# Retention in chunks of 64 tokens on 64x64 tiles of the array, with the inner and the state products issued apart

## Chip, cores and metric

One core of a Trainium2 chip runs the program. The metric is the device time in microseconds of one execution. TensorE (PE, its weight loads PEld), VectorE (DVE), ScalarE (ACT), GpSimd (POOL) and SyncE (SP) each run a queue of their own; the queues meet at semaphores only.

## The reference

Four sequences of 1024 tokens with 1024 features. Of the normalized rows `xn` it computes a retention layer with 16 heads of 64, and a linear layer whose input and weights are rounded to 4 bits in blocks of 16, and adds both to `x`:

```python
q = heads((x @ Wq + bq) * scaling); k = heads(x @ Wk + bk); v = heads(x @ Wv + bv)
D = jnp.where(causal[None], jnp.exp(decay[:, None, None] * diff_c[None]), 0.0)
ret = jnp.einsum('bhid,bhjd->bhij', q, k) * D[None]
scale = jnp.clip(jnp.abs(jax.lax.stop_gradient(ret).sum(-1, keepdims=True)), 1.0, None)
attn = jnp.einsum('bhij,bhjd->bhid', ret / scale, v)
...
g = (g - mu) / jnp.sqrt(var + EPS)      # per head, over its 64 features
g = g.reshape(b, s, e) * gn_w + gn_b
gate = jax.nn.silu(x @ Wg + bg)
return gate * g @ Wo + bo
...
x = x + attention(xn) + ffn(xn)
```

Since the weight of a pair of tokens decays by a constant factor per token, the sum over earlier tokens can be split: tokens of the same chunk are multiplied out (scores, then inner products with v), and all tokens of earlier chunks enter through a 64x64 state per head that is decayed and increased by each chunk (state products).

## The kernel before

The 4096 tokens are cut into 8 groups of 512, a group into 4 chunks of 128 (CH). The weights are in pairs of heads: 8 pairs, 128 features each. A **body** computes two pairs (u = 0, 1) of one group, and the output rows and the next group's input of one chunk. There are 2 + 2 bodies of the phases FIRST_A and FIRST_B (together group 0), 4 of SECOND (group 1), 24 of MIDDLE (groups 2 to 7) and 4 of TAIL. Every group has 4 bodies. `parity` is the group's number modulo 2; groups with parity 0 begin a sequence, and their first chunk has no state before it.

In a body PE runs, for each pair, four projections (`project`, L1145: k, v, q and g, n = 0 to 3, each 24 matmuls of 512 columns in f16 parts, into the PSUM banks mm0 and mm1 in turn), transposes of k and v (`transpose_kv`, L1159), the scores (L1167, 24 f16 matmuls of 128x128 blocks with 64 rows of contraction, one head in each half of the rows), the state increments (L1178, f32, k decayed times v with a column of ones), and `attend` (L1190): the state products (L1203, q times the state before the chunk) and the inner products (L1207, masked scores times v) into the same banks `ao`. P(u,n) below is the projection n of pair u. `transpose_g` (L1122, Tg below) transposes the group-normalized output. From group 1 on there are also `finish_half` (L1093, the output projection of the group before, 24 matmuls) and in MIDDLE `finish_linear` (L1114, 8 matmuls).

The other engines, in the order of their queues in a body:

- ACT (L651 to L679): copies of k(0) and v(0) out of mm (`evacuate`, L593, lines L604 and L606), `decay_k(0)`, `x_hi`, copy of q(0), `copy_v(0)`, g(0), k(1), v(1), `decay_k(1)`, `normalize(0)` (L632, line L637), q(1), `copy_v(1)`, g(1), `affine(0)` (L642, line L647), `normalize(1)`, `affine(1)`. `affine(1)` waits for Tg of pair 1, which PE issues in the next body, `transpose_g(1, 1)` at L1215.
- DVE (L991 to L1037): layer norm and quantizing of one input chunk, `mask_scores(0)` (L929), `states(0)` (L938), `group_norm(0)` (L954), `mask_scores(1)`, `states(1)`, the output additions, `group_norm(1)`, output additions.
- POOL: `split` (L450) makes the second f16 part of k and q, `decay_q`, `gate_y`.
- SP issues all DMAs: one slice of weights ahead of each projection, inputs, outputs and transposing DMAs.

The order is written out by hand, and all waits are counts in the table PER. `group_norm(u)` waits for `attn_full`, which the last matmul of `attend` raises; `normalize(u)` waits for `gstats`; scores(1) waits for `kq_split`, which POOL raises after q(1) has been copied by ACT; `transpose_kv(0, "k")` waits for `mm0_free`, raised by ACT's second copy of k.

Of the kernel before, what the change touches and what calls it, by code (L numbers as in the profile page):

```python
# [52 lines left out]
VW = HD + 1  # L53
BLK = 16
# [24 lines left out]
    "attn_full": (1, 2, 2, 2, 2, 0), "gstats": (0, 2, 2, 2, 2, 0), "normed": (1, 2, 2, 2, 2, 0),  # L79
# [13 lines left out]
    "step": (85, 74, 74, 120, 76, 0),  # L93
# [53 lines left out]
def build(nc, a):  # L147
    with ExitStack() as ctx:
# [15 lines left out]
        dmask = sb("dmask", [P, HEADS, P])  # L164
# [22 lines left out]
        state = sb("state", [P, CH, VW])  # L187
# [47 lines left out]
        bias_sum = ctx.enter_context(nc.semaphore("bias_sum"))  # L235
        v_ones = ctx.enter_context(nc.semaphore("v_ones"))
# [16 lines left out]
        late_res = probs[:].rearrange("p a b c -> p (a b c)")  # L253
        block = ctx.enter_context(nc.Block())
# [6 lines left out]
        def _(sp):  # L261
# [19 lines left out]
            for dst, name in ((ident[:], "ident"), (dec_h[:], "dec_h"),  # L281
                              (dec_c[:], "dec_c"), (work[:, 0:P], "ages"), (xa[:, 0:P], "causal"),
# [235 lines left out]
        def _(act):  # L518
# [4 lines left out]
            for h in range(HEADS):  # L523
                nc.scalar.activation(dmask[:, h, :], work[:, 0:P], ACT.Exp, scale=dec_h[:, h:h + 1])
# [3 lines left out]
            nc.scalar.activation(lam[:], dec_c[:], ACT.Exp, scale=float(P)).then_inc(tables, 1)  # L528
# [157 lines left out]
        def _(dve):  # L686
# [196 lines left out]
            then(V.tensor_scalar(xa[:, 0:P], xa[:, 0:P], kq_down["k"], kq_down["q"], ALU.mult, ALU.mult))  # L883
            V.tensor_scalar(kfac[:], kfac[:], kq_down["k"], None, ALU.mult)
            V.tensor_scalar(qfac[:], qfac[:], kq_down["q"], None, ALU.mult)
            then(V.tensor_tensor(dmask[:], dmask[:], xa[:, 0:P].unsqueeze(1).broadcast_to([P, HEADS, P]), ALU.mult))
# [22 lines left out]
            def body(phase, i, parity, q, group):  # L909
# [19 lines left out]
                def mask_scores(u):  # L929
                    w("scores_full", u + 1)  # L930
                    w("attn_full", u)
                    for h in range(2):
                        factor = dmask[:, ds(q * 4 + 2 * u + h, 1), :].broadcast_to([P, CH, P])
                        last = V.tensor_tensor(probs[:, h], sc[h].rearrange("p (c t) -> p c t", c=CH), factor,  # L934
                                               ALU.mult)
                    last.then_inc(s["probs_ready"], 1)

                def states(u):  # L938
# [5 lines left out]
                    if parity == 0:  # L944
                        then(V.tensor_copy(state[:, 1], tp[bk][:, 0:VW]))
# [5 lines left out]
                    V.scalar_tensor_tensor(pair, state[:, CH - 1], decay, tp[bk][:, (CH - 1) * VW:CH * VW],  # L951
# [46 lines left out]
                if phase == SECOND:  # L998
                    f_scales(0)
                    f_half(0)  # L1000
# [309 lines left out]
```

## Time and profile before

| | us |
|---|---|
| median of 3 runs | 2363.78 (2360.42 to 2365.61) |
| the profiled execution's own time | 2367.02 |
| its span, first to last instruction | 2365.2 |
| PE busy | 2186.9 (92%) |
| DVE busy | 1451.8 (61%) |
| ACT busy | 672.8 (28%) |
| POOL busy | 635.1 (27%) |

The profile's page has busy times by engine, a row of 40 slices, the chain that ended last and the costliest groups of instructions. Two more views are used: windows, which give the same numbers for chosen stretches with the granted clock of TensorE (PEclk, 1.00 is 2.4 GHz, 0.50 is 1.2 GHz), and the timeline, which lists the instructions of an engine with their start, their duration, and in brackets how long the engine had been idle before and what released it. An f32 matmul leaves two records. Durations of matmuls overlap, so a rate is read from one start to a later start.

### The profile page before, as it was taken

Reading aid. Unit: us, or ns where it says so; the run is one execution under the profiler, and the core shown is the slowest. Engines: PE = TensorE matmul, PEld = TensorE weight load, DVE = VectorE, ACT = ScalarE, POOL = GpSimd, SP = SyncE. Lnnn points to the kernel's source line nnn. Section 1 sums busy time; section 2 is a strip of 40 time slices with the busy share of each in tenths; the row PEclk is TensorE's granted clock in tenths of the full one; section 3 lists DMA queues with packets and bytes.
Section 4 is the critical chain, followed back from the end, with each engine's and each line's share of the span. In section 5 each row is a group of like instructions: output and inputs, shape, how many; then the busy total and the mean of one; then the engine's idle time right before and its main releaser. Section 6 shows DMA issues by size and latency. Waiting matters only on the chain.

```text
span 2365.2 us, 42202 instructions
## 1 busy us (share of the span) xinstructions
PE 2186.9 (92%) x13472; PEld 1158.0 (49%) x13472; DVE 1451.8 (61%) x4086; ACT 672.8 (28%) x1259; POOL 635.1 (27%) x460
## 2 busy tenths in 40 slices
PE   1289797988889999999999999999999999999999
PEld 1044453544445555555555555555555555555554
DVE  7766576887974555666655555666655556666532
ACT  4534332222222223222222223222222223222220
POOL 1022232222222233223222233232222233232321
PEclk9689899898989999999999999999999999999999
DMA  7964333234323233333233233333233233333233
GB/s 284 368 202 148 94 114 104 85 98 126 104 76 103 86 105 111 103 103 102 82 96 103 83 108 111 103 103 102 77 101 102 81 111 111 103 102 99 78 102 116
DMA packets 189396, 271.20 MB, mean 115 GB/s; under 512 B 118288, under 2 KB 139280, under 8 KB 188304
## 3 DMA queue, kind: packets, MB, share of 16 engines
q1 hardware_dynamic: 189328, 270.35, 36.6%
q8 instruction: 36, 0.59, 0.1%
q14 instruction: 32, 0.26, 0.0%
HBM read 203.20 MB, written 37.75 MB: 102 GB/s over the span
## 4 chain that ended last, share of the span: by engine, by line
PE 79%; DVE 13%; issue 2%; SPq 2%; ACT 2%; DMA 1%; POOL 0%; DVEq 0%; ACTq 0%; POOLq 0%
PE mm L1154 48%; PE mm L1101 6%; PE tp L1101 6%; PE four L1207 5%; PE mm L1110 4%; PE four L1203 3%; PE tp L1164 2%; PE four L1174 2%; PE tp L1186 1%; SPq L277 1%; PE tp L1128 1%; DVE xm L753 1%; DVE xa L750 1%; DVE xa L755 1%; DVE xa L751 1%
## 5 line engine op out<-in xcount | busy, mean ns | idle before, releaser
L1154 PE MATMUL mm<-xnT,wring 128*128 128x512 f16 x6144 | 1391.4, 384 | 47.8 <-ACT qT L606 15.5
L1154 PEld LDWEIGHTS mm<-xnT,wring 128*128 128x128 f16 x6144 | 604.7, 99 | 753.9 <-issue 54.3
L637 ACT ACTIVATE work<-four,gs 128x64 f32<-128x64 f32 x512 | 158.0, 414 | 545.5 <-DVE gs L976 545.5
L934 DVE TENSOR_TENSOR probs<-four,dmask 128x512 f32<-128x512 f32 x128 | 82.5, 686 | 325.5 <-PE four L1174 324.2
L470 POOL TENSOR_TENSOR yT<-gn,gate 128x512 f32 x64 | 81.2, 1269 | 659.3 <-ACT gn L647 659.3
L453 POOL TENSOR_TENSOR qparts<-qT,qparts 128x512 f16<-128x512 f32 x64 | 79.8, 1247 | 657.0 <-ACT qT L606 657.0
L963 DVE BATCH_NORM_STATS2 gst<-four 128x6 f32<-128x64 f32 x512 | 73.6, 217 | 230.3 <-PE four L1207 229.5
L1101 PE MATMUL mm<-wo,yT 128*128 128x512 f16 x864 | 192.6, 379 | 0.0
L1101 PE MATMUL tp<-wo,yT 128*128 128x512 f16 x672 | 149.6, 379 | 0.0
L453 POOL TENSOR_TENSOR kparts<-kT,kparts 128x512 f16<-128x512 f32 x64 | 76.8, 1199 | 224.6 <-ACT kT L606 209.5
L1207 PE MATMUL four<-v,probs 128*128 128x65 f32 x1024 | 136.7, 290 | 0.0
L1207 PEld LDWEIGHTS four<-v,probs 128*128 128x128 f32 x1024 | 127.6, 203 | 4.6
L1101 PEld LDWEIGHTS mm<-wo,yT 128*128 (+1 forms) x864 | 82.2, 98 | 96.5 <-POOL yT L473 0.4
L606 ACT ACTIVATE vT<-mm,bias,cols 128x512 f32<-128x512 f32 x64 | 49.7, 777 | 238.1 <-PE mm L1154 238.1
L606 ACT ACTIVATE gate<-mm,bias,cols 128x512 f32<-128x512 f32 x64 | 49.7, 777 | 193.9 <-PE mm L1154 193.9
L1101 PEld LDWEIGHTS tp<-wo,yT 128*128 (+1 forms) x672 | 66.1, 100 | 73.6
L755 DVE TENSOR_TENSOR xa<-xa,xm 128x512 f32<-128x512 f32 x80 | 100.4, 1255 | 2.8
L1203 PE MATMUL four<-state,qT 64*128 64x65 f32 x896 | 68.0, 291 | 35.4 <-DVE carry L951 35.4
L1110 PE MATMUL mm<-wf,xqT 128*128 128x512 bf16 x416 | 98.3, 379 | 0.0
L604 ACT ACTIVATE kparts<-mm,bias,cols 128x512 f16<-128x512 f32 x64 | 49.5, 773 | 168.7 <-PE four L1174 168.6
L647 ACT ACTIVATE gn<-tp,gnp 128x512 f32<-128x512 f32 x64 | 49.5, 773 | 161.1 <-PE tp L1128 161.1
L621 ACT ACTIVATE kn<-tp,kfac 128x256 f32<-128x256 f32 x128 | 53.4, 470 | 132.8 <-PE tp L1164 132.8
(174 smaller groups left out, 2483.5 us busy)
## 6 DMA issues: line engine op xcount, KB each, us to landing
wring<-parts SPq DMA_DIRECT2D x256, 512.0 KB, 3.4
xt<-in_x SPq DMA_DIRECT2D x34, 512.0 KB, 4.3
out<-res SPq DMA_DIRECT2D x32, 512.0 KB, 2.9
res<-in_x SPq DMA_DIRECT2D x28, 512.0 KB, 3.5
parts<-xqT SPq DMA_DIRECT2D x36, 256.0 KB, 4.4
parts<-xnT SPq DMA_DIRECT2D x36, 256.0 KB, 3.5
ftile<-in_w_f SPq DMA_DIRECT2D x16, 512.0 KB, 4.3
yT<-in_w_k SPq DMA_DIRECT2D x1, 4096.0 KB, 14.8
```

The lines of the kernel that those rows point to most:

```text
L453: nc.gpsimd.tensor_tensor(parts[:, 1], full[:], parts[:, 0], ALU.subtract)\
L470: nc.gpsimd.tensor_tensor(hi, gn[:], gate[:, u], ALU.mult)
L606: nc.scalar.activation(dst, mm[n % 2][:], ACT.Silu if n == 3 else ACT.Identity, bias=bias[:, n, pair(u)], scale=down[MATS[n]])\
L637: last = nc.scalar.activation(work[:, c * P + h * HD:c * P + (h + 1) * HD], ao[h][:, c * VW:c * VW + HD], ACT.Identity, bias=gs[:, 1, g:g ...
L755: then(V.tensor_tensor(xa[:], xa[:], xm[:], ALU.add))
L934: last = V.tensor_tensor(probs[:, h], sc[h].rearrange("p (c t) -> p c t", c=CH), factor, ALU.mult)
L963: last = V.bn_stats(gst[:, g, :], ao[h][:, c * VW:c * VW + HD])
L1101: last = MM(out[:], y[:, yj, k, ds(q * P, P)], wo[:, wj, k, h * GROUP:(h + 1) * GROUP], start=(n == 0), stop=(n == 3 * KT - 1))
L1110: last = MM(out, xs[:, k, :], wf[:, k, h * GROUP:(h + 1) * GROUP], start=(k == 0), stop=(k == KT - 1))
L1154: last = MM(mm[n % 2][:], wring[:, slot, wj, k, :], xnT[:, parity, xj, k, :], start=(j == 0), stop=(j == 3 * KT - 1))
L1203: MM(ao[h][:, columns(c)], qT[r, c * P:(c + 1) * P], state[r, c], start=(c == earlier[0]), stop=False, skip_group_check=True)
L1207: last = MM(ao[h][:, columns(c)], probs[:, h, c, :], v1[:, c, h, :], start=False, stop=True, skip_group_check=True)
```

## The change

The chunk of the attention shrinks from 128 to 64 tokens (SUB, 8 per group), while all copies keep their layout of 128. Scores, masks, increments, state products and inner products all use 64x64 tiles: two token halves times two heads. The inner products and the state products become two functions, `attend_within` and `attend_earlier`, which raise `within` and `attn_full`. Half of the increments are written to the free half of the banks of the scores, so they wait for the mask (`probs_ready`). PE's order changes: P(0,1) precedes the transposes of g of the body before, the increments and inner products of pair 0 follow P(1,1), its state products follow P(1,2); in pair 1 the scores precede the output half, and the state products follow the second output half. On DVE the recurrence has 8 steps, and in SECOND and FIRST the mask and the states change places with parts of the weight quantizing. ACT's and POOL's queues keep their order.

```diff
-        dmask = sb("dmask", [P, HEADS, P])
+        dmask = sb("dmask", [P, HEADS, SUB])
...
+        def increment(bk, k):
+
+            c = k // 2
+            if k % 2 == 0:
+                return tp[bk][:, c * VW:(c + 1) * VW]
+            first = CH * SUB + c % 2 * VW
+            return sc[c // 2][:, first:first + VW]
...
-                    for c in range(1 if parity == 0 else 0, CH - 1):
-                        then(V.scalar_tensor_tensor(state[:, c + 1], state[:, c], decay, tp[bk][:, c * VW:(c + 1) * VW],
+                    for k in range(1 if parity == 0 else 0, SUBS - 1):
+                        then(V.scalar_tensor_tensor(state[:, k + 1], state[:, k], decay, increment(bk, k),
                                                     ALU.mult, ALU.add))
...
+                mask_scores(0)
+                if phase == SECOND:
                     f_half(0)
-                mask_scores(0)
-                states(0)
                 if phase in FIRST:
                     find_f_max(0)
+                states(0)
...
                 def scores(u):
                     w("kq_split", 2 * u + 2)
                     w("probs_ready", u)
+                    pe.sem_inc(pe_turn, 1)
                     for c in range(CH):
-                        for h in range(2):
-                            r, t = slice(h * HD, (h + 1) * HD), slice(c * P, (c + 1) * P)
-                            for kj, qj in ((0, 0), (0, 1), (1, 0)):
-                                last = MM(sc[h][:, t], kparts[r, kj, t], qparts[r, qj, t],
-                                          start=(kj + qj == 0), stop=(kj == 1))
+                        for kj, qj in ((0, 0), (0, 1), (1, 0)):
+                            for par in range(2):
+                                for h in range(2):
+                                    r, out = slice(h * HD, (h + 1) * HD), slice(par * SUB, (par + 1) * SUB)
+                                    at_t = slice(c * P + par * SUB, c * P + (par + 1) * SUB)
+                                    last = MM(sc[h][out, c * SUB:(c + 1) * SUB], kparts[r, kj, at_t],
+                                              qparts[r, qj, at_t], start=(kj + qj == 0), stop=(kj == 1))
...
+                    w("probs_ready", u + 1)
+                    pe.sem_inc(pe_turn, 1)
+                    for k in range(SUBS):
+                        rows, c = slice(k % 2 * SUB, (k % 2 + 1) * SUB), k // 2
                         for h in range(2):
-                            last = MM(tp[bk][h * HD:(h + 1) * HD, c * VW:(c + 1) * VW], kn[:, c, h, :], v1[:, c, h, :],
+                            last = MM(increment(bk, k)[h * HD:(h + 1) * HD], kn[rows, c, h, :], v1[rows, c, h, :],
                                       start=True, stop=True)
...
+                def attend_within(u):
+                    w("normed", u)
+                    pe.sem_inc(pe_turn, 1)
+                    for k in range(SUBS):
+                        for h in range(2):
+                            last = MM(ao[h][tokens(k), columns(k)], probs[tokens(k), h, k // 2, 0:SUB],
+                                      v1[tokens(k), k // 2, h, :], start=(k < 2), stop=False, skip_group_check=True)
+                    last.then_inc(s["within"], 1)
+
+                def attend_earlier(u):
                     w("qdec_ready", u + 1)
...
+                    for k in range(1 if parity == 0 else 0, SUBS):
                         for h in range(2):
                             r = slice(h * HD, (h + 1) * HD)
+                            last = MM(ao[h][tokens(k), columns(k)], qT[r, k * SUB:(k + 1) * SUB], state[r, k],
                                       start=False, stop=True, skip_group_check=True)
                     last.then_inc(s["attn_full"], 1)
...
                 project(0, 0)
+                project(0, 1)
                 if last_g:
                     transpose_g(1, 1)
-                project(0, 1)
                 transpose_kv(0, "k", kT, 0)
...
                 scores(0)
+                project(1, 1)
                 state_increments(0)
-                project(1, 1)
-                attend(0)
+                attend_within(0)
                 transpose_kv(1, "k", kT, 0)
                 project(1, 2)
+                attend_earlier(0)
                 transpose_kv(1, "v", vT, 1)
-                project(0 if phase in FIRST else 1, 3)
-                transpose_g(0)
+                if phase in FIRST:
+                    scores(1)
+                    project(0, 3)
+                    state_increments(1)
+                    attend_within(1)
+                    project(1, 3)
+                    transpose_g(0)
+                    attend_earlier(1)
+                    return
+                project(1, 3)
                 scores(1)
-                state_increments(1)
-                if phase in FIRST:
-                    project(1, 3)
-                    attend(1)
-                    return
                 pe.wait_ge(s["y_ready"], group * (2 * CH) + 1)
                 finish_half(w, parity, q, 0, "mm0", 5)
+                transpose_g(0)
+                state_increments(1)
+                attend_within(1)
                 if phase == MIDDLE:
                     finish_linear(w, parity, q, 0, "mm1", 5)
-                attend(1)
-                if phase == MIDDLE:
                     finish_half(w, parity, q, 1, "t1", 4)
-                    finish_linear(w, parity, q, 1, "mm1", 6)
                 else:
                     finish_half(w, parity, q, 1, "mm1", 5)
+                attend_earlier(1)
+                if phase == MIDDLE:
+                    finish_linear(w, parity, q, 1, "mm1", 6)
```

How the rows of PE move. The start of a MIDDLE body before (`work` is the normalized output that Tg transposes, `xnT,wring` a projection; ISA and REGISTER_ALU rows compute the counts waited for):

```order
L1154 MATMUL mm<-xnT,wring 128x512 x24
L257 ISA
L257 REGISTER_ALU
L1128 MATMUL tp<-ident,work 128x128 x4
L257 REGISTER_ALU
L257 ISA
L1154 MATMUL mm<-xnT,wring 128x512 x24
L257 REGISTER_ALU x2
L1164 MATMUL tp<-ident,kT 128x128 x4
```

and of the change:

```order
L1169 MATMUL mm<-xnT,wring 128x512 x24
L269 REGISTER_ALU
L269 ISA
L1169 MATMUL mm<-xnT,wring 128x512 x24
L269 ISA
L269 REGISTER_ALU
L1143 MATMUL tp<-ident,work 128x128 x4
L269 REGISTER_ALU x2
L1179 MATMUL tp<-ident,kT 128x128 x4
L1169 MATMUL mm<-xnT,wring 128x512 x24
```

The transposes of g (L1128, now L1143) stood between the two projections and now stand directly ahead of those of kT.

Pair 0 of a MIDDLE body from its state products on, before (scores(1), L1174, come next):

```order
L1203 MATMUL four<-state,qT 128x65 x8
L1207 MATMUL four<-v,probs 128x65 x8
L257 REGISTER_ALU
L1164 MATMUL tp<-ident,kT 128x128 x4
L1154 MATMUL mm<-xnT,wring 128x512 x24
L257 REGISTER_ALU
L1164 MATMUL tp<-ident,vT 128x128 x4
L257 REGISTER_ALU
L1154 MATMUL mm<-xnT,wring 128x512 x24
L257 REGISTER_ALU
L1128 MATMUL tp<-ident,work 128x128 x4
L257 REGISTER_ALU
```

and the same place of the change, from the inner products on:

```order
L1219 MATMUL four<-v,probs 64x65 x16
L269 REGISTER_ALU
L1179 MATMUL tp<-ident,kT 128x128 x4
L1169 MATMUL mm<-xnT,wring 128x512 x24
L269 REGISTER_ALU
L1232 MATMUL four<-state,qT 64x65 x16
L269 REGISTER_ALU
L1179 MATMUL tp<-ident,vT 128x128 x4
L269 REGISTER_ALU
L1169 MATMUL mm<-xnT,wring 128x512 x24
L269 REGISTER_ALU
L1192 MATMUL four<-qparts,kparts 64x64 x48
```

The state products (L1203, now L1232) stood ahead of the inner products and of the projection of q(1); now they follow that projection, and between them and scores(1) only vT and one projection are left.

## Rows read from the trace of the kernel before

**Rows 1.** The page, section 1, busy time by engine, share of span, instructions.
```profile
PE 2186.9 (92%) x13472; PEld 1158.0 (49%) x13472; DVE 1451.8 (61%) x4086; ACT 672.8 (28%) x1259; POOL 635.1 (27%) x460
```

**Rows 2.** Windows: stretch, length, busy time by engine (x instructions), PEclk, DMA share, GB/s.
```profile
365.00:689.40 324.40, 274.72 (x1623) 148.43 (x1621) 259.46 (x680) 76.98 (x156) 80.87 (x57) 0.89 0.33 99
689.40:2290.00 1600.60, 1600.60 (x10078) 848.66 (x10079) 930.61 (x2791) 444.00 (x885) 462.22 (x336) 1.00 0.33 98
...
1041.41:1108.24 66.83, 66.83 (x426) 35.54 (x424) 39.66 (x118) 18.55 (x38) 19.29 (x14) 1.00 0.33 98
...
1308.27:1374.65 66.38, 66.38 (x418) 35.12 (x416) 38.51 (x118) 18.55 (x38) 19.28 (x14) 1.00 0.33 99
```

**Rows 3.** Timeline of PE, a FIRST body: start, us, engine, line, count, [idle before].
```profile
311.99 0.66 PE L1128 MATMUL tp<-ident,work 128*128 128x128 f32 x4 [2.52 <-ACT work L637]
```

**Rows 4.** Timeline of PE, pair 0 of one MIDDLE body.
```profile
1051.71 0.85 PE L1174 MATMUL four<-qparts,kparts 64*128 64x128 f16 x24
1052.49 0.69 PE L1186 MATMUL tp<-v,kn 128*64 128x65 f32 x16
1053.11 5.35 PE L1154 MATMUL mm<-xnT,wring 128*128 128x512 f16 x24
1058.39 1.11 PE L1203 MATMUL four<-state,qT 64*128 64x65 f32 x16
1059.43 2.00 PE L1207 MATMUL four<-v,probs 128*128 128x65 f32 x16
1061.27 0.61 PE L1164 MATMUL tp<-ident,kT 128*128 128x128 f32 x4
1061.71 5.34 PE L1154 MATMUL mm<-xnT,wring 128*128 128x512 f16 x24
1066.89 0.60 PE L1164 MATMUL tp<-ident,vT 128*128 128x128 f32 x4
...
1073.04 0.85 PE L1174 MATMUL four<-qparts,kparts 64*128 64x128 f16 x24
```

**Rows 5.** Timelines of PE and ACT, start of the next body.
```profile
1096.41 0.60 PE L1128 MATMUL tp<-ident,work 128*128 128x128 f32 x4
...
1097.16 0.78 ACT L647 ACTIVATE gn<-tp,gnp 128x512 f32<-128x512 f32 x1 [5.36 <-PE tp L1128]
1097.84 0.77 ACT L604 ACTIVATE kparts<-mm,bias,cols 128x512 f16<-128x512 f32 x1
1098.50 0.77 ACT L606 ACTIVATE kT<-mm,bias,cols 128x512 f32<-128x512 f32 x1
```

**Rows 6.** Timelines of DVE, ACT and POOL, between the pairs.
```profile
1061.46 1.15 DVE L963 BATCH_NORM_STATS2 gst<-four 128x6 f32<-128x64 f32 x8 [5.82 <-PE four L1207]
...
1066.27 2.47 ACT L637 ACTIVATE work<-four,gs 128x64 f32<-128x64 f32 x8 [3.42 <-DVE gs L976]
1068.59 0.82 ACT L604 ACTIVATE qparts<-mm,bias,cols 128x512 f16<-128x512 f32 x1
...
1070.15 1.16 POOL L453 TENSOR_TENSOR qparts<-qT,qparts 128x512 f16<-128x512 f32 x1 [12.40 <-ACT qT L606]
```

**Rows 7.** Timeline of PE and windows, around three idles in SECOND.
```profile
644.90 1.97 PE L1203 MATMUL four<-state,qT 64*128 64x65 f32 x16 [4.25 <-DVE carry L951]
...
527.58 5.35 PE L1154 MATMUL mm<-xnT,wring 128*128 128x512 f16 x24 [2.03 <-DVE res L1045]
...
604.89 1.65 PE L1154 MATMUL mm<-xnT,wring 128*128 128x512 f16 x6 [2.03 <-DVE res L1045]
...
643.60:653.80 10.20, 8.90 (x43) 7.04 (x44) 8.06 (x33) 0.84 (x2) 0.00 (x0) 0.50 0.31 78
...
527.60:531.00 3.40, 3.40 (x16) 1.56 (x17) 3.23 (x7) 1.64 (x6) 0.00 (x0) 1.00 0.38 154
...
604.90:609.50 4.60, 4.60 (x14) 1.80 (x15) 4.36 (x9) 1.65 (x6) 0.00 (x0) 0.63 0.28 114
```

**Rows 8.** Groups of DVE by line: busy us, mean ns | idle before.
```profile
L949 DVE SCALAR_TENSOR_TENSOR state<-state,lam,tp 128x65 f32<-128x65 f32 x160 | 45.1, 282 | 14.3 <-DVE state L945 4.7 <-DVE state L947 3.1 <-DVE state L949 0.2
```

More of the change, by code:

```diff
@@ L53 @@
 VW = HD + 1
+SUB = 64
+SUBS = GROUP // SUB
 BLK = 16
@@ L91 @@
     "w_k": (2, 2, 2, 2, 2, 0), "w_v": (2, 3, 3, 2, 2, 0), "w_q": (2, 2, 2, 2, 2, 0), "w_g": (2, 1, 1, 2, 2, 0),
-    "step": (85, 74, 74, 120, 76, 0),
+    "step": (85, 82, 82, 128, 84, 0),
 }
@@ L186, in build @@
         probs = sb("probs", [P, 2, CH, P])
-        state = sb("state", [P, CH, VW])
+        state = sb("state", [P, SUBS, VW])
         gn = sb("gn", [P, GROUP])
@@ L523, in _ @@
             for h in range(HEADS):
-                nc.scalar.activation(dmask[:, h, :], work[:, 0:P], ACT.Exp, scale=dec_h[:, h:h + 1])
+                nc.scalar.activation(dmask[:, h, :], work[:, 0:SUB], ACT.Exp, scale=dec_h[:, h:h + 1])
             for r in range(PAIRS):
@@ L1012, in body @@
                 mask_scores(1)
-                states(1)
+                if phase == SECOND:
+                    f_half(0)
                 if phase == FIRST_B:
                     split_o_lo(i, 1, w)
-                if phase == SECOND:
-                    f_half(0)
+                states(1)
                 if phase == MIDDLE:
@@ L1116, in finish_linear @@
                 w(f"{bank}_free", use - 1)
+                pe.wait_ge(s["xqf_moved"], at("xqf_moved", MIDDLE, 0, 0))
                 linear(banks[bank][:], parity, q, h).then_inc(s[f"{bank}_full"], 1)
@@ L1191, in attend @@
+                def attend_earlier(u):
                     w("qdec_ready", u + 1)
-                    w("probs_ready", u + 1)
                     b, n = uses[f"u{u}"]
                     w(f"t{b}_free", n)
-                    w("normed", u)
-                    earlier = [c for c in range(CH) if not (parity == 0 and c == 0)]
-                    columns = lambda c: slice(c * VW, (c + 1) * VW)
-                    for c in earlier:
+                    w("within", u + 1)
+                    pe.sem_inc(pe_turn, 1)
+                    for k in range(1 if parity == 0 else 0, SUBS):
@@ L1201, in attend @@
                         for h in range(2):
                             r = slice(h * HD, (h + 1) * HD)
-                            MM(ao[h][:, columns(c)], qT[r, c * P:(c + 1) * P], state[r, c],
-                               start=(c == earlier[0]), stop=False, skip_group_check=True)
-                    for c in range(CH):
-                        for h in range(2):
-                            last = MM(ao[h][:, columns(c)], probs[:, h, c, :], v1[:, c, h, :],
+                            last = MM(ao[h][tokens(k), columns(k)], qT[r, k * SUB:(k + 1) * SUB], state[r, k],
@@ L1253, in _ @@
             run_phase(pe, SECOND, body)
-            pe.wait_ge(s["xqf_moved"], at("xqf_moved", MIDDLE, 0, 0))
             run_phase(pe, MIDDLE, body)
@@ L1277 @@
     idx = np.arange(P)
+    sub = idx % SUB
     decay = g[p + "decay"]
@@ L1293 @@
         "ident": np.eye(P, dtype=f32),
-        "ages": np.maximum(idx[None, :] - idx[:, None], 0).astype(f32),
-        "causal": (idx[None, :] >= idx[:, None]).astype(f32),
-        "pos": np.broadcast_to(idx.astype(f32), (P, P)).copy(),
-        "left": (P - idx).astype(f32).reshape(P, 1),
+        "ages": np.maximum(sub[None, :SUB] - sub[:, None], 0).astype(f32),
+        "causal": (sub[None, :SUB] >= sub[:, None]).astype(f32),
+        "pos": np.broadcast_to(sub.astype(f32), (P, P)).copy(),
+        "left": (SUB - sub).astype(f32).reshape(P, 1),
     }
```

24 lines of the change are left out of this document (13 added, 11 removed).

## The prediction

> **What bounds the kernel now.** I read the page first, then stretches, then one body instruction by instruction. TensorE is busy 92% of the span [rows 1]. By stage [rows 2]: from 689.4 us to 2290.0 us (the 24 MIDDLE bodies) PE is busy for all of its 1600.60 us at clock 1.00, and DVE for 58%. One body takes 66.83 us (odd groups) or 66.38 us (even), 66.6 in the mean. So in MIDDLE every microsecond of PE work counts fully, and so does every wait that PE is made to take. In the four SECOND bodies (most of 365.0 to 689.4) PE is busy 274.72 of 324.40 us and DVE 259.46: there DVE and PE wait for each other. In the FIRST bodies PE waits for ACT, as at 311.99 [rows 3].
>
> The sum is made against the profiled execution, 2367.0 us with a span of 2365.2; it stands 3.2 us above the median of 2363.8. A difference of 0.2% (some 5 us) is about what a measurement here can tell from none.
>
> **The attention products.** The timeline of PE in one body [rows 4] gives what a pair costs. A projection without a change of tile shape takes 5.18 us (1061.71 to 1066.89), so the one begun at 1053.11 is through at 1058.29, and the state products start at 1058.39: a change of tile shape costs 0.10. From start to next start: scores 0.78 for 24 records, increments 0.62 for 16, state products 1.04 for 16, inner products 1.84 for 16 (an f32 matmul leaves two records). The first three include one change of shape each, and there are two more, going into scores and into the state products: 4.28 + 0.20 = 4.48 us a pair, of which 0.5 are five changes and 3.98 is work.
>
> That work runs in steps. Scores use two 64-row tiles at once: 12 steps of 0.057. Increments use two 64-column tiles at once: 8 steps of 0.065. State products, two 64-row tiles with 128 columns of weights: 8 steps of 0.118. Inner products, the whole array with 128 columns of weights: 16 steps of 0.115. The step follows the weight columns, not the rows.
>
> The change makes 48, 32, 32 and 32 records, 144 for 72. All have 64 columns of weights. No row has four tiles at once, so it is bounded. Taken: four tiles work abreast where the code addresses four in turn, and a step costs what the nearest row with 64 weight columns shows. Scores 12 x 0.057 = 0.68; increments 8 x 0.065 = 0.52 (as many as before, with twice the records and twice the tiles); state products 8 x 0.065 = 0.52; the inner products only ever use the two tiles on the diagonal, 16 x 0.065 = 1.04. Together 2.76, and six changes of shape for five (there are three stretches of 64x64 tiles a pair, each entered from and left to the 128x128 shape): 0.60. 3.36 for 4.48 saves 1.12 us a pair, **2.2 us a body**. The lower end of the cost is every step halved once more, 1.4 + 0.6 = 2.0 (5 us saved a body). The upper end is that no record comes faster than the closest ones do now, scores with 0.68/24 = 0.028 us: 144 x 0.028 + 0.6 = 4.6, nothing saved.
>
> The Trainium skill, TensorEngine Tiling (Array Packing), section Instruction Overhead, speaks against such small pieces: about 60 cycles for each matmul whatever its width, and a tiling factor should not be taken from a side that is already small. Estimated from that page, 60 cycles at 2.4 GHz are 25 ns, so 144 records would take 3.6 us and the sum would save 0.3 us a pair in place of 1.1; no row here has narrow tiles four abreast to settle it.
>
> **The transposes of g, moved behind P(0,1).** Before, Tg (L1128) stands between the first two projections. ACT must then run affine and both copies of k before PE may transpose kT, because they stand in this order in its queue, and the queue is not changed. The rows [rows 5]: Tg from 1096.41, 0.44 long for PE; affine 1097.16, kparts 1097.84, kT from 1098.50 to 1099.27. That ran under the second projection. Now kT's transposes follow Tg at once: they could start at Tg's start + 0.44 and are allowed 1099.27 - 1096.41 = 2.86 later at the earliest. Idle **2.5 us** a body with the hand-over. Nothing else covers it: the ACT queue is strictly ordered, and affine cannot precede Tg.
>
> **The state products of pair 0, moved behind P(1,2).** They now carry attn_full, on which group norm waits. ACT holds normalize(0) ahead of the copies of q of pair 1, these release POOL's split, and scores(1) waits for the split. This chain [rows 6], from the end of the attention at 1061.27 (kT's start, [rows 4]): group norm 1061.46, normalize 1066.27, q copies from 1068.59, split 1070.15 to 1071.31, **10.04 us**. Before, PE had kT, P(1,2), vT, P(1,3) and Tg to do meanwhile (scores(1) came at 1073.04, 1.7 us of slack). Now only a change of shape 0.10, vT 0.44 and P(1,3) 5.18 remain, 5.72. Idle 10.04 - 5.72 = 4.3, with hand-overs **4.4 us** a body, at most 5. In FIRST nothing but vT stands between, so the idle is 9.4 there.
>
> **The clock.** An idle PE here loses clock. At 644.90 PE had been idle for 4.25 us, and the 10.20 us from 643.60 were granted 0.50, which is 1.2 GHz, with 8.90 busy [rows 7]: 4.4 us lost. After two idles of 2.03 us the clock was 1.00 once and 0.63 over 4.60 us once (1.7 lost). For the kT idle I take 1.5. For the scores idle 3.1, between 1.7 and 4.4, since mostly dense 512-column matmuls follow here where small ones followed at 644.90. Together **4.6 us** a body.
>
> **Cheap or covered edits.** The state recurrence grows by 4 steps a pair of 0.282 us [rows 8], 2.3 us a body on DVE, which is busy 39.66 of 66.83 us; P(1,2) lies over it. The masks halve in width, a gain on DVE that nothing waits for. increments(0) later by P(1,1): its readers are the state products, now 5.6 us further on. emit_linear frees mm1 after group norm(1), which starts later; the chain 0.2 + 4.8 + 1.5 from the state products' end, less the linear's 1.9, ends 4.6 after the body's start, and P(0,1) needs it at 5.2: covered, by only 0.6 us. No DMA is added or moved in SP's or POOL's queue; SP is released later by PE alone. In SECOND the mask now stands ahead of a half of the weight quantizing, which takes away PE idles such as those of 4.25.
>
> **The sum.** MIDDLE: -2.2 + 2.5 + 4.4 + 4.6 = +9.3 a body, times 24 = +223. SECOND: PE's own path is 63.1 (without the two linears of 8 matmuls each, 5.18/24 apiece, 3.5) + 9.3 = 72.4, still under the present pace of about 81 us; taken that half of the two waits shows, +5 x 4 = +20. FIRST: 9.4 + 2 (kT) + 3 (clock) - 2.2 - 2.5 (the idle at 311.99 goes, since P(1,3) now precedes Tg) = +10, a little more in two bodies with a weight copy in ACT's chain: +42. Start and tail about 0. +285 on 2367: **2652 us**.
>
> **Rivals.**
> - Tiles that do not pack: a step per record as in the upper end, or only two of four tiles at once. For it: no row shows four. Against: pairs do overlap in scores, increments and state products. The idles stay. 1.2 to 1.3 us a pair more than forecast, 64 pairs, +81: 2733, and up to 2800 where both hold. This is also the case in which the change does not do what it says. Chance 0.22.
> - The waits come without the loss of clock: 24 x 4.6 + 8 x 3 = 134 less, 2518. For it: one of two short idles left the clock alone. Against: the long one did not. Chance 0.07.
> - The other side, faster: the copies of q do not have to wait for the state products, the chain of [rows 6] runs under PE, and only tile savings remain, 2367 - 64 x 1.12 = 2295. It decides once the chain is shorter than 5.7 + 1.1 us, and kT's is gone as well; group norm alone takes 4.8. Only a misreading of ACT's queue gives it. Chance 0.02.
> - Forecast: chance 0.69.
>
> The range, 2565 to 2785, takes in tile steps halved (64 x 1.4 = 87 less) and most of the first rival; outside are the second and third, and the far end of the first. Faster 0.02, same 0.01, slower 0.97.
>
> **What would show it.** Right: in a MIDDLE body, about 76 us long, PE idles of 2.5 us at the transposes of kT <- ACT kT, and of 4 to 5 at scores <- POOL qparts; clock about 0.9 in MIDDLE; a pair's attention work 2.8 us without changes of shape; ACT's work row still released by DVE gs. Wrong: MIDDLE bodies under 67 us, no idle at these two places, or the idle elsewhere, as at mm1 for P(0,1).

## The result, and the profile after

| | before | after |
|---|---|---|
| median us | 2363.22 (2360.42 to 2365.61, 4 runs) | 2611.45 (2608.23 to 2611.9, 4 runs) |
| profiled execution us | 2367.02 | 2611.76 |
| its span us | 2365.2 | 2610.0 |
| granted clock, mean | 0.967 | 0.918 |

The changed kernel takes 1.105 times the time of before (95% interval 1.103 to 1.107), 248 us more. The forecast was 2652, the range 2565 to 2785.

First the page of the changed kernel: TensorE's busy time by engine, then groups (busy us, mean ns of one | idle before them and what ended it).

```profile
PE 2205.7 (85%) x18029; PEld 1094.8 (42%) x18080; DVE 1489.7 (57%) x4342; ACT 671.6 (26%) x1259; POOL 639.2 (24%) x460
...
L1192 PE MATMUL four<-qparts,kparts 64*64 64x64 f16 x3072 | 45.9, 217 | 162.6 <-POOL qparts L465 162.6
...
L1179 PE MATMUL tp<-ident,kT 128*128 128x128 f32 x256 | 53.8, 345 | 105.6 <-ACT kT L618 105.6
```

PE is busy 85% of a longer span where it was 92% [rows 1], with 18.8 us more of busy time although it has less to do. The two groups that stand ahead of idle time are the two the prediction named: the scores (L1192), released by POOL's split of q, 162.6 us, and the transposes of kT (L1179), released by ACT's copy of k, 105.6 us. Of those 105.6 us, 30.1 are one wait at the start of the program, which the kernel before has too (31.5 there); the 24 MIDDLE bodies hold 57.4 (24 x 2.39).

Next windows (columns as in [rows 2]): SECOND of the kernel before, then of the changed kernel SECOND, MIDDLE, one MIDDLE body, and two short pieces of it.

```profile
362.70:689.40 326.70, 277.02 (x1634) 149.51 (x1634) 261.45 (x695) 76.98 (x156) 80.87 (x57) 0.89 0.33 100
...
397.50:724.20 326.70, 264.15 (x2208) 130.40 (x2208) 251.21 (x703) 75.66 (x153) 84.35 (x60) 0.91 0.33 99
724.20:2529.60 1805.40, 1637.78 (x13488) 815.85 (x13537) 966.05 (x2989) 444.40 (x886) 468.97 (x336) 0.93 0.28 87
...
1027.70:1102.80 75.10, 68.11 (x567) 33.99 (x568) 40.98 (x127) 18.55 (x37) 19.29 (x14) 0.93 0.30 89
1040.90:1044.20 3.30, 3.12 (x10) 1.66 (x11) 3.16 (x5) 2.51 (x5) 3.11 (x4) 0.50 0.14 55
1081.90:1088.60 6.70, 5.53 (x60) 2.48 (x61) 0.76 (x2) 0.95 (x2) 2.29 (x2) 0.50 0.02 5
```

MIDDLE takes 1805.40 us where it took 1600.60 [rows 2], and PE is busy for 1637.78 of them, no longer for all. SECOND takes 326.70 us. It took as long before (the first row). The last two windows show the clock at 0.50, which is 1.2 GHz: for 3.3 us from just before the first of the two idles ends (1041.08), and for 6.7 us around the end of the second, 1.2 before PE starts again at 1083.07 and 5.5 after.

The timeline of PE in that body (start us, us, instruction, [idle before]) answers to [rows 4] and the first row of [rows 5]:

```profile
1038.09 0.60 PE L1143 MATMUL tp<-ident,work 128*128 128x128 f32 x4
1041.08 1.11 PE L1179 MATMUL tp<-ident,kT 128*128 128x128 f32 x4 [2.39 <-ACT kT L618]
1041.99 6.43 PE L1169 MATMUL mm<-xnT,wring 128*128 128x512 f16 x24
1048.25 0.60 PE L1179 MATMUL tp<-ident,vT 128*128 128x128 f32 x4
...
1059.14 0.58 PE L1192 MATMUL four<-qparts,kparts 64*64 64x64 f16 x48
1059.68 5.35 PE L1169 MATMUL mm<-xnT,wring 128*128 128x512 f16 x24
1064.96 0.28 PE L1207 MATMUL tp<-v,kn 64*64 64x65 f32 x2
...
1065.47 1.15 PE L1219 MATMUL four<-v,probs 64*64 64x65 f32 x32
1066.56 0.66 PE L1179 MATMUL tp<-ident,kT 128*128 128x128 f32 x4
1067.05 5.34 PE L1169 MATMUL mm<-xnT,wring 128*128 128x512 f16 x24
...
1072.33 0.70 PE L1232 MATMUL four<-state,qT 64*64 64x65 f32 x32
1072.95 0.66 PE L1179 MATMUL tp<-ident,vT 128*128 128x128 f32 x4
1073.45 5.34 PE L1169 MATMUL mm<-xnT,wring 128*128 128x512 f16 x24
1083.07 0.86 PE L1192 MATMUL four<-qparts,kparts 64*64 64x64 f16 x48 [4.28 <-POOL qparts L465]
1083.86 7.66 PE L1115 MATMUL mm<-wo,yT 128*128 128x512 f16 x24
1091.35 0.60 PE L1143 MATMUL tp<-ident,work 128*128 128x128 f32 x4
```

Pair 0 stands from 1059.14 to 1072.95. After it come vT, P(1,3) from 1073.45, and then an idle of 4.28 us before scores(1). At the head of the body PE is done with Tg (1038.09) after 0.44 and cannot start kT before 1041.08. Both waits are there, at the two places and by the two releasers that were forecast. The chain behind the second one, on DVE, ACT and POOL in turn, answers to [rows 6]:

```profile
1073.09 1.15 DVE L976 BATCH_NORM_STATS2 gst<-four 128x6 f32<-128x64 f32 x8 [4.39 <-PE four L1232]
...
1077.89 2.47 ACT L649 ACTIVATE work<-four,gs 128x64 f32<-128x64 f32 x8 [9.69 <-DVE gs L989]
1080.21 0.81 ACT L616 ACTIVATE qparts<-mm,bias,cols 128x512 f16<-128x512 f32 x1
...
1081.77 1.15 POOL L465 TENSOR_TENSOR qparts<-qT,qparts 128x512 f16<-128x512 f32 x1 [16.85 <-ACT qT L618]
```

From the end of the state products, 1072.95, to the end of the split, 1081.77 + 1.15 = 1082.92, are 9.97 us; [rows 6] gave 10.04.

### The profile page after: what moved, and what is told of

It reads as the page before. It is cut to its first block, busy times and chain, and to the rows that moved or that the text cites. A ratio compares the mean times of both kernels' runs of the same rounds, so it can differ in the third digit from the quotient of the medians.

```text
span 2610.0 us, 52065 instructions
## 1 busy us (share of the span) xinstructions
PE 2205.7 (85%) x18029; PEld 1094.8 (42%) x18080; DVE 1489.7 (57%) x4342; ACT 671.6 (26%) x1259; POOL 639.2 (24%) x460
## 4 chain that ended last, share of the span: by engine, by line
PE 40%; issue 38%; POOL 11%; DVE 5%; ACT 3%; SPq 1%; DMA 1%; POOLq 1%; ACTq 0%; DVEq 0%
PE mm L1169 16%; PE mm L1115 10%; PE tp L1115 6%; PE mm L1124 3%; POOL qparts L465 3%; POOL xhl L490 3%; POOL res L497 2%; POOL kparts L465 2%; POOL gate L483 1%; PE four L1219 1%; SPq L289 1%; PE tp L1143 1%; PE four L1192 1%; ACT gn L659 1%; PE four L1232 1%
## 5 line engine op out<-in xcount | busy, mean ns | idle before, releaser
L1169 PE MATMUL mm<-xnT,wring 128*128 128x512 f16 x6144 | 1416.7, 390 | 60.4 <-DVE res L1059 22.7
L1115 PE MATMUL mm<-wo,yT 128*128 128x512 f16 x864 | 255.8, 467 | 0.0
L946 DVE TENSOR_TENSOR probs<-four,dmask 128x256 f32<-128x256 f32 x128 | 48.3, 419 | 255.5 <-PE four L1192 254.2
L1192 PE MATMUL four<-qparts,kparts 64*64 64x64 f16 x3072 | 45.9, 217 | 162.6 <-POOL qparts L465 162.6
L1115 PEld LDWEIGHTS mm<-wo,yT 128*128 (+1 forms) x864 | 97.8, 117 | 143.7 <-issue 82.9
L1179 PE MATMUL tp<-ident,kT 128*128 128x128 f32 x256 | 53.8, 345 | 105.6 <-ACT kT L618 105.6
L1192 PEld LDWEIGHTS four<-qparts,kparts 64*64 64x64 f16 x3072 | 39.0, 129 | 190.0 <-issue 190.0
L1124 PE MATMUL mm<-wf,xqT 128*128 128x512 bf16 x368 | 87.9, 379 | 7.6 <-issue 7.6
L472 POOL TENSOR_TENSOR qT<-qT,qfac 128x512 f32<-128x512 f32 x64 | 81.7, 1276 | 12.6 <-POOL qparts L465 12.6
L483 POOL TENSOR_TENSOR gate<-gn,gate 128x512 f32<-128x512 f32 x64 | 83.6, 1306 | 0.0
```

The lines of the kernel that those rows point to most:

```text
L472: nc.gpsimd.tensor_tensor(qT[:].rearrange("p (c t) -> p c t", c=CH), qT[:].rearrange("p (c t) -> p c t", c=CH), factor, ALU.mult).then_inc ...
L483: nc.gpsimd.tensor_tensor(gate[:, u], gn[:], gate[:, u], ALU.mult).then_inc(s["gated"], 1)
L1115: last = MM(out[:], y[:, yj, k, ds(q * P, P)], wo[:, wj, k, h * GROUP:(h + 1) * GROUP], start=(n == 0), stop=(n == 3 * KT - 1))
L1124: last = MM(out, xs[:, k, :], wf[:, k, h * GROUP:(h + 1) * GROUP], start=(k == 0), stop=(k == KT - 1))
L1169: last = MM(mm[n % 2][:], wring[:, slot, wj, k, :], xnT[:, parity, xj, k, :], start=(j == 0), stop=(j == 3 * KT - 1))
L1192: last = MM(sc[h][out, c * SUB:(c + 1) * SUB], kparts[r, kj, at_t], qparts[r, qj, at_t], start=(kj + qj == 0), stop=(kj == 1))
```

## The experiments

Two theories were set against each other. **Mine**: the 248 us are two waits of PE made by the new order (kT behind ACT, scores(1) behind group norm, normalize and POOL) and the half clock after each of them, while the tiles themselves save a little. **The rival**: the small tiles cost the time (more than twice the records, more changes of shape), or the waits cost what they cost and the clock is no separate matter. One kernel puts the old tiles under the new order; two undo one wait each, and one both; two fill a wait with work for PE that nobody needs; one has the old tiles under the mended order; and the last goes a step on from the best. All but the first and the seventh have the tiles of the change.

**1. The new order with the old tiles.** Chunks of 128 tokens and the tile shapes of before. The products are only split into an inner and an earlier part and put in the order of the change, and DVE's order is that of the change too. The cut shows part of the edit.

```diff
@@ before, PE's order
-                project(0, 0)
-                if last_g:
-                    transpose_g(1, 1)
-                project(0, 1)
+                project(0, 0)
+                project(0, 1)
+                if last_g:
+                    transpose_g(1, 1)
...
-                attend(0)
+                attend_within(0)
                 transpose_kv(1, "k", kT, 0)
                 project(1, 2)
+                attend_earlier(0)
                 transpose_kv(1, "v", vT, 1)
```

> The new order of PE (and of DVE) with the old chunks of 128 tokens and their tile shapes. Theory (the order costs, the tiles save): the change's time plus what its tiles save, 1.42 us a pair read from its trace, times 64 pairs: 2611 + 91 = 2702, range 2680 to 2715, with idles of 2.5 us at the kT transposes and 4.3 us at scores(1) as in the change. Rival (the small tiles are what costs, more matmuls and more changes of shape): about 2365 to 2450, without these idles. Second rival (PE waits anyway, so the tiles' saving no longer counts): 2611 to 2625.

Measured: 2669.51 us (2667.46 to 2671.68), 1.128 of before (1.127 to 1.130). PE's timeline in one MIDDLE body:

```profile
1221.99 0.66 PE L1167 MATMUL tp<-ident,kT 128*128 128x128 f32 x4 [2.39 <-ACT kT L607]
1222.48 5.34 PE L1157 MATMUL mm<-xnT,wring 128*128 128x512 f16 x24
...
1263.86 1.03 PE L1177 MATMUL four<-qparts,kparts 64*128 64x128 f16 x24 [4.19 <-POOL qparts L454]
1264.81 6.81 PE L1103 MATMUL mm<-wo,yT 128*128 128x512 f16 x24
```

Both waits are there with the tiles of before, 2.39 and 4.19 us. So they come from the order, and the small tiles do not make them: the order alone costs 306 us against before, more than the whole change. The total lies 10 us under the range I had set. The tiles save 58 us under this order, less than the 69 to 104 that this range stood for. Here the clock falls in fewer of the bodies (mean clock 0.937, against 0.918 in the change), so the two kernels differ in more than the tiles: from the start of kT to that of vT a MIDDLE body takes 5.67 us at clock 1.00, as the body shown does, and over 7.1 where the clock fell, which is so in 8 of the 24 bodies here and in all 24 of the change. Why it falls in fewer was not taken apart.

**2. The copies of q ahead of normalize(0).** One move in ACT's queue. The copies then only wait for the state products of pair 0, which read the q that they overwrite.

```diff
                 decay_k(1)
+                w("attn_full", 1)
+                evacuate(1, 2)
+                copy_v(1)
                 normalize(0)
                 if phase == FIRST_B:
                     split_o_hi(i, 1)
-                evacuate(1, 2)
-                copy_v(1)
```

> The change with one move in ACT's queue: the copies of q(1) and v(1) wait for attn_full themselves and then come ahead of normalize(0). Theory (the chain group norm, normalize, q copies, split holds scores(1)): the idle of 4.34 us at scores(1) goes and with it 2.56 us of clock, 6.9 us a MIDDLE body, 166 us; FIRST loses its longer idle, some 30 us; SECOND stays near its pace: 2415, range 2390 to 2440, the idle at kT stays. Rival (DVE with its longer recurrence or the mask holds PE there): the idle moves to another matmul and the time stays above 2560.

Measured: 2410.18 us (2406.8 to 2414.18), 1.018 of before (1.016 to 1.020), 201 us under the change.

```profile
1116.63 1.11 PE L1180 MATMUL tp<-ident,kT 128*128 128x128 f32 x4 [2.40 <-ACT kT L618]
...
1148.52 0.66 PE L1180 MATMUL tp<-ident,vT 128*128 128x128 f32 x4
...
1154.28 0.58 PE L1193 MATMUL four<-qparts,kparts 64*64 64x64 f16 x48
1154.83 5.35 PE L1116 MATMUL mm<-wo,yT 128*128 128x512 f16 x24
```

scores(1) now starts at 1154.28, with no idle, 5.27 us after P(1,3) as any projection does. The finish_half behind it takes its ordinary time (5.35 us for 24 matmuls, where the change's took 7.66). The wait for kT is left as it was, 2.40, and the clock still falls there in all 24 MIDDLE bodies. So the wait at scores(1) hung on the place of normalize in ACT's queue and on nothing that the tiles do.

**3. Tg back between P(0,0) and P(0,1).**

```diff
                 project(0, 0)
-                project(0, 1)
                 if last_g:
                     transpose_g(1, 1)
+                project(0, 1)
```

> The change with the transposes of g back between P(0,0) and P(0,1). Theory: the idle of 2.55 us at the kT transposes and its 1.56 us of clock go, but the transposes of g now wait for normalize(1), 0.5 to 1.5 us, since the state products of pair 1 end late: 3.3 us a body net, 24 bodies and a little in the others: 2535, range 2515 to 2560; the idle at scores(1) stays. Rival (the order of these two makes no difference, the wait for normalize(1) is as long as the one for kT): 2600 to 2615.

Measured: 2525.83 us (2523.29 to 2528.65), 1.067 of before (1.065 to 1.069), 86 us under the change.

```profile
1162.05 0.65 PE L1143 MATMUL tp<-ident,work 128*128 128x128 f32 x4 [0.45 <-ACT work L649]
...
1167.71 0.60 PE L1179 MATMUL tp<-ident,kT 128*128 128x128 f32 x4
...
1208.15 0.86 PE L1192 MATMUL four<-qparts,kparts 64*64 64x64 f16 x48 [4.28 <-POOL qparts L465]
1208.94 7.66 PE L1115 MATMUL mm<-wo,yT 128*128 128x512 f16 x24
```

kT follows its projection at once. Tg now waits 0.45 us itself for ACT's normalize(1). The other wait keeps its 4.28 us and its half clock (finish_half 7.66).

**4. Both moves**, the edits of 2 and 3 together.

> Both moves together, with the tiles and everything else of the change. Theory: what is left is the tiles' saving of 2.8 us a body less the short wait at the transposes of g, and the clock stays at 1.00: 2335, range 2320 to 2355, faster than the kernel before (2363). Rival (the two idles cover each other, or a third wait takes their place): 2400 or more.

Measured: 2323.29 us (2322.9 to 2324.8), 0.982 of before (0.980 to 0.984).

```profile
1144.09 0.65 PE L1144 MATMUL tp<-ident,work 128*128 128x128 f32 x4 [0.45 <-ACT work L649]
...
1149.76 0.60 PE L1180 MATMUL tp<-ident,kT 128*128 128x128 f32 x4
```

The one idle in this body is the 0.45 at Tg. From 1138.30 to 1203.10, 64.80 us, the clock is 1.00. The two moves singly gave 201 and 86, 287 in all; together they give 288. So the two gains add up. With its waits mended the change is 40 us faster than before.

**5. The wait at scores(1) filled with unused work.** 18 matmuls of 512 columns whose result nobody reads, in MIDDLE. They take the time of the wait and let nothing start earlier.

```diff
+                def filler(n):
+                    for _ in range(n):
+                        MM(sc[0][:], wo[:, 0, 0, 0:P], wo[:, 0, 0, 0:GROUP], start=True, stop=True)
...
                 project(1, 3)
+                if phase == MIDDLE:
+                    filler(18)
                 scores(1)
```

> The change with 18 extra 512-column matmuls (3.9 us at full clock, fixed operands, result unused) in MIDDLE ahead of scores(1), where PE would be idle for 4.3 us. The wait itself stays. Theory (of the 6.9 us a body that this place costs, 2.56 are lost clock): granted clock 1.00 behind the place, 2.56 us a body less, 24 bodies: 2550, range 2535 to 2570. Rival (the slower matmuls behind the idle come from something else, such as refilling PE's queue): 2605 to 2620.

Measured: 2530.55 us (2527.72 to 2531.2), 1.070 of before (1.068 to 1.073), 81 us under the change with more work in it, and 4 under the range I had set. Timeline of PE, then windows around this place (the second) and around kT's transposes in three bodies that follow each other (the others):

```profile
1204.51 4.05 PE L1184 MATMUL four<-wo 128*128 128x512 f16 x18
1208.96 0.57 PE L1196 MATMUL four<-qparts,kparts 64*64 64x64 f16 x48 [0.41 <-POOL qparts L465]
1209.53 5.35 PE L1115 MATMUL mm<-wo,yT 128*128 128x512 f16 x24
```

```profile
1166.00:1174.00 8.00, 5.61 (x29) 2.82 (x29) 7.55 (x14) 4.57 (x7) 5.27 (x4) 1.00 0.35 142
1204.30:1216.00 11.70, 11.29 (x137) 5.77 (x136) 0.75 (x2) 4.98 (x12) 2.42 (x2) 1.00 0.14 45
1236.00:1244.00 8.00, 5.61 (x23) 2.87 (x22) 7.62 (x12) 4.58 (x7) 5.26 (x4) 0.79 0.46 188
1308.00:1316.00 8.00, 5.61 (x31) 2.93 (x30) 7.55 (x12) 4.57 (x7) 4.77 (x4) 1.00 0.49 196
```

The filler runs through the wait, scores(1) starts no sooner behind its projection, and the body is shorter all the same: the clock is 1.00 through scores and finish_half. That is 24 x 2.56 = 61 us given back. The other 20 were not expected. At kT, where nothing was changed and PE still idles 2.40 us, the clock was 1.00 in the first and the third body and 0.79 over 8 us in the one between them. The same idle costs clock after some bodies and not after others. From kT to vT, 9 of the 24 MIDDLE bodies take over 7.1 us and 15 take 5.67, where the change takes over 7.1 in all 24. 15 x 1.5 = 23 us, which covers the 20. What decides whether a body loses its clock was not found: experiment 2 has no idle at scores(1) either, and loses it at kT in every body.

**6. The wait at kT filled**, 9 such unused matmuls ahead of the transposes of kT in MIDDLE.

```diff
+                if phase == MIDDLE:
+                    filler(9)
                 transpose_kv(0, "k", kT, 0)
```

> The same with 9 extra matmuls (1.9 us) ahead of the transposes of kT, in the idle of 2.5 us. Theory: 1.56 us of clock a body come back, 2574, range 2560 to 2590; the idle itself stays filled. Rival: 2605 to 2620.

Measured: 2565.13 us (2562.34 to 2566.85), 1.084 of before (1.082 to 1.087), 46 us under the change. 24 x 1.55 = 37 was the clock's price at this place. The rest came back at the other place, where nothing was changed: scores(1) and the first finish_half take 7.7 us in the mean of the 24 bodies (7.0 to 8.6), and 8.3 in the change. PE's waits for kT fall from 105.6 us to 59.6, as 24 idles do that a filler of about 2 us covers.

**7. The order with both moves and the old tiles.** Experiment 1 with the edits of 2 and 3.

> The new order with the moves of e4 (q copies ahead of normalize, transposes of g back) and the old chunks of 128. Here nothing idles long enough to lose clock, so the distance to e4 is the tiles' saving alone. Theory: 1.42 us a pair, 64 pairs, less what SECOND hides: 2323 + 80 = 2403, range 2390 to 2415. Rival (the tiles save the 58 us that separate the change from e1, 0.9 a pair): 2375 to 2385.

Measured: 2397.16 us (2395.01 to 2401.12), 1.014 of before (1.012 to 1.017). Against experiment 4, where the order is the same and only the tiles differ, the small tiles save 74 us, 1.15 us a pair over 64 pairs. That is the cleanest price of the tiles, since both kernels run the inside of MIDDLE (725 to 2250 and 725 to 2200 us) at a granted clock of 1.00. Most of it falls in MIDDLE, where a body takes 67.74 us here and 64.80 in experiment 4 in odd groups, 67.29 and 64.75 in even ones. Against before, whose MIDDLE also runs at 1.00, the mended order alone is 1.4% slower: 67.74 stand against 66.83, and about 0.65 of these 0.9 us are the late transposes of g.

**8. One more step from experiment 4.** In MIDDLE the state products of pair 1 come ahead of the second finish_half, so that group norm(1) and normalize(1) are through when Tg needs them.

```diff
                 if phase == MIDDLE:
                     finish_linear(w, parity, q, 0, "mm1", 5)
+                    attend_earlier(1)
                     finish_half(w, parity, q, 1, "t1", 4)
                 else:
                     finish_half(w, parity, q, 1, "mm1", 5)
-                attend_earlier(1)
+                    attend_earlier(1)
```

> e4 with the state products of pair 1 in MIDDLE ahead of the second output half in place of behind it, so that normalize(1) is done when the transposes of g come. Theory: the wait of 0.45 us there and the short one ahead of it go, 24 x 0.5 to 1.0 us less than e4: 2305, range 2295 to 2315. Rival (the state products now wait for the eight steps of the recurrence for as long as is gained): 2318 to 2335.

Measured: 2311.76 us (2311.38 to 2313.38), 0.978 of before (0.976 to 0.980), the fastest of all.

```profile
1062.33 0.60 PE L1144 MATMUL tp<-ident,work 128*128 128x128 f32 x4
...
1066.73 0.70 PE L1233 MATMUL four<-state,qT 64*64 64x65 f32 x32 [0.37 <-DVE carry L965]
```

The idle at Tg is gone from the bodies, which take 64.3 to 64.7 us. A smaller one came in its place, 0.37 in odd groups and 0.10 in even ones: the state products, earlier by a projection, now wait for DVE's carry. With it the gain is 11.5 us and not the 18 expected.

## Why the prediction was right, and where it was off

The case forecast, two waits and their clock against a small saving of the tiles, is the one that came. By stages (from where each begins to where the next does) the terms compare as follows.

| stage | forecast us | measured us |
|---|---|---|
| FIRST | +42 | +35 |
| SECOND | +20 | 0 |
| MIDDLE | +223 (24 x 9.3) | +204.8 |
| TAIL | 0 | +5 |
| sum | +285 | +245 |

In one MIDDLE body that has all its state products, 66.83 us before [rows 2] and 75.10 now:

| term | forecast us | measured us | by |
|---|---|---|---|
| tiles | -2.2 | -2.7 | below |
| wait at kT | +2.5 | +2.55 | 1038.09 + 0.44 to 1041.08 |
| wait at scores(1) | +4.4 | +4.34 | 1073.45 + 5.28 to 1083.07 |
| clock, kT's place | +1.5 | +1.55 | 1041.08 to 1048.25 is 7.17 for 5.62 |
| clock, scores' place | +3.1 | +2.56 | 1083.07 to 1091.35 is 8.28 for 5.72 |

These sum to +8.3, and 66.83 + 8.3 = 75.1.

**The waits.** Right in place, releaser and size. The chain through ACT's queue came out at 9.97 us for the 10.04 read off before. A queue whose order is fixed can be read like this ahead of time: take the chain from the trace of before, and lay beside it what PE has left to do meanwhile.

**The tiles.** Right in kind, and mis-sized in one step. From start to next start, pair 0 of the body above: scores 0.54, increments 0.51, inner products 1.09, state products 0.62. A projection ahead of a stretch of 64x64 tiles takes 5.27 or 5.28 for 5.18, which is the change of shape on entering. Scores, inner and state products contain the one on leaving, taken at the same 0.10; that leaves 0.44, 0.51, 0.99 and 0.52, 2.46 of work, and with six changes, 0.60, it is 3.06. Three were forecast well at a step of 0.065. The scores were not: "12 x 0.057 = 0.68", and twelve steps of four tiles took 0.44, 0.037 each. The step of scores had been read where a weight tile is 128 columns wide, and its own was less than that of the f32 products. One thing was in no count: kT behind the inner products and vT behind the state products take 0.49 each (1066.56 to 1067.05) where [rows 4] has 0.44, 0.10 a pair. So a pair costs some 3.15 and not 3.36, and saves 1.3 to 1.4 of its 4.48, 2.7 a body; the 1.42 and 2.8 of the expectations leave those 0.10 out. In an even group, whose first chunk has no earlier state, 0.4 a body less is saved. Before, the state products that fall away there shortened a pair from 1.04 to 0.82; now they shorten it from 0.63 (32 records) to 0.61 (28), since those of the first 64 tokens ran beside those of the second. So the body is 75.1 us long in odd and even groups alike, where it was 66.83 and 66.38.

The other price that I had given, added up by record, falls with this. 48 records of the scores in 0.44 us are 9 ns each. The Trainium skill, TensorEngine Tiling (Array Packing), section Instruction Overhead, has about 60 cycles for each matmul, 25 ns at 2.4 GHz by the estimate in the prediction, which would be 1.2 us here. The trace does not agree with that rule, counted for each matmul, where tiles run four abreast. (In the prediction I also counted records for matmuls: an f32 matmul leaves two, so the 144 records are 96 matmuls.) The first rival, tiles that do not pack, falls too: its upper end needs 0.028 us a record for all 144, and they took 0.009 in scores, 0.016 in increments and state products, and 0.031 only in the inner products, which use two tiles and were forecast at 0.033.

**The clock.** Right in kind; 4.1 us a body for 4.6. At scores I took 3.1 "between 1.7 and 4.4"; it was 2.56. The second rival, waits without loss of clock, is out by experiment 5: there the wait's time stayed and only the clock came back, 81 us. What I had no term for is that the loss at one place is not the same in every kernel or body, though the idle is. It gave experiment 5 its 20 us more than its place was worth. It also bears on the 58 us between the change and experiment 1, against the 74 between experiments 4 and 7: a MIDDLE body of experiment 1 takes 76.2 us in the mean, 1.1 over the change, with clock lost at kT in a third of them and less of it lost at scores(1); without any loss of clock the distance is 2.7 (67.5 and 64.8).

**SECOND, the term that missed most.** It said that half of the two waits shows, +5 x 4 = +20, and it counted nothing for the new order on DVE beyond that. PE's waits in SECOND (engine and line <- releaser: us in all, times, longest), before:

```profile
PE four L1203 <- DVE carry L951: 29.0, 4, 13.8
PE mm L1154 <- DMA wf<-xqf: 10.7, 1, 10.7
```

and in the change:

```profile
PE four L1192 <- POOL qparts L465: 18.5, 4, 4.8
PE mm L1169 <- DVE res L1059: 17.0, 3, 5.7
PE tp L1179 <- ACT kT L618: 9.6, 4, 2.4
```

The waits did come, 18.5 at scores and 9.6 at kT. What went are the 29.0 us in which the state products of before waited for DVE's carry: DVE masks the scores of pair 0 ahead of half of the quantizing now, and the products come a projection later. I had named those idles as going, and put no number on it. How much the new waits cost after that shows in the kernels with the two moves. From scores(0) of the first SECOND body to scores(0) of the first MIDDLE body, before takes 323.4 us (395.98 to 719.36), the change 322.9 (435.72 to 758.66), and experiment 4 307.4 (405.43 to 712.81). So the two waits and their clock cost 15.5 in SECOND, near the 20, and the new order and tiles give back 16 that the sum did not have. Experiment 7, with the old tiles, takes 308.2 (412.03 to 720.25): the gain is the order's, not the tiles'. Which of the moves on DVE and PE makes it was not taken apart.

**FIRST and TAIL.** In FIRST the idle at scores(1) was forecast at 9.4, and more where a weight copy stands in ACT's chain; here is such a body:

```profile
381.93 0.86 PE L1192 MATMUL four<-qparts,kparts 64*64 64x64 f16 x48 [11.32 <-POOL qparts L465]
```

Of the 7 us between +42 and +35 the tiles' larger saving, 0.5 a body, makes 2; the rest was not taken apart. TAIL was put at 0 and lost 5: its only Tg, at the head of the stage with no projections before it, waits for normalize(1), since the state products of pair 1 now come at the very end of the last MIDDLE body.

```profile
2535.36 0.74 PE L1143 MATMUL tp<-ident,work 128*128 128x128 f32 x4 [3.83 <-ACT work L649]
```

**The third rival**, faster than before because the copies of q need not wait for the state products, needed a misreading of ACT's queue, and there was none. But what it described is close to what experiments 2 to 4 made by hand, and its 2295 is near the 2312 of experiment 8.

**What stays open.** Why the same idle at kT costs clock in all 24 MIDDLE bodies of the change and of experiment 2, in 9 of them in experiment 5 and in 8 in experiment 1. And whether the fillers of experiments 5 and 6 gave back clock by their activity alone, or also by moving later work in time.

## What to carry to other kernels

Before moving a product in one engine's order, follow the queue of the engine that reads it, and lay the chain from its new end to the next instruction that needs a buffer or a copy beside the work PE has left: here 10.0 us against 5.7 made a wait of 4.3 in each body, and putting two copies ahead of a normalization in ACT's queue took it away for 201 of the 248 us. An idle PE can cost more than its length (in the change 1.55 us of half clock after 2.4 idle, 2.56 after 4.3), so a short wait in a dense loop can be worth more than it looks. Small tiles paid (74 us), and were hidden under an order that cost four times as much: time such a change with the order held still, and then the other way round.

## What the runs showed of the hardware

- Four 64x64 tiles of the array, addressed in turn, work abreast: 48 records of the scores (f16, 64 columns) took 0.44 us, 9 ns a record, where 24 records over two 64x128 tiles took 0.68. In the trace their starts come in fours within 10 to 13 ns, some 32 ns from one four to the next. By the rate of a projection (5.18 us for 24 matmuls of 512 columns) 64 columns take 27 ns, an estimate, so at 9 ns a record at least three must run at once. For f32 with 65 columns a step took the same time with twice the records in it: 0.51 us for the 32 records of the increments on four tiles, 0.52 for 16 on two.
- A change of tile shape cost 0.10 us on entering (a projection takes 5.27 to 5.28 for 5.18), with 64x64 tiles as with the shapes of before. The Trainium skill, TensorEngine Tiling (Array Packing), section Key Properties, says that changing the mode drains the array; a delay of 0.10 us fits that, though no row shows the drain itself.
- The loss of clock after an idle is not a property of that idle alone. With the wait at scores filled, the same 2.40 us at kT were followed by a granted clock of 1.00 in one body and of 0.79 over 8 us in the next; time was lost there in 9 of 24 MIDDLE bodies. In the change, with both idles in each body, 0.50 followed both of them in the body shown, and all 24 lost time at kT; so did all 24 of experiment 2, where the idle at scores is gone.
